# A narrow attention's stacks through DRAM: parts side by side, 12 reads of 4 KB rows and 6 writes a batch in place of 32 reads and one write

## The reference, cut to what matters

```python
def _L3_xattn_ref(query, key, value, Wq, bq, Wk, bk, Wv, bv, Wo, bo):
    EMBED_DIM, NUM_HEADS = 128, 16
    HEAD_DIM = EMBED_DIM // NUM_HEADS
    q = (query @ Wq.T + bq).reshape(b, tq, NUM_HEADS, HEAD_DIM).transpose(0, 2, 1, 3)
    k = (key @ Wk.T + bk).reshape(b, tk, NUM_HEADS, HEAD_DIM).transpose(0, 2, 1, 3)
    v = (value @ Wv.T + bv).reshape(b, tk, NUM_HEADS, HEAD_DIM).transpose(0, 2, 1, 3)
    scores = jnp.einsum('bhqd,bhkd->bhqk', q, k) / np.sqrt(HEAD_DIM)
    attn = jax.nn.softmax(scores, axis=-1)
    out = jnp.einsum('bhqk,bhkd->bhqd', attn, v)
    return out.transpose(0, 2, 1, 3).reshape(b, tq, EMBED_DIM) @ Wo.T + bo
```

## Time and profile before

| what | value |
|---|---|
| time, median of 3 runs | 2500.98 us (2495.63 to 2509.0) |
| the profiled execution | 2520.08 us, its span 2518.3 us, mean granted TensorE clock 0.896 |
| busy | TensorE 79% of the span, VectorE 61%, ScalarE 52%, GpSimd 20% |
| transfers scratch<-parts (L1408) | 768 of 32 KB |
| transfers parts<-scratch (L1398) | 24 of 384 KB, median 2.6 us from issue to landing |
| the three narrow attentions, first write issued at | 376.17, 1085.53 and 2177.64 us |

### The profile page before, as it was taken

One profiled execution on the slowest core, in us unless ns is written; L12 is line 12 of the kernel. 1 busy time (PEld: TensorE's weight loads), 2 busy tenths in 40 slices (PEclk: granted clock), 3 DMA queues, 4 the chain that ended last, 5 costly groups with the idle time before them and its releaser, 6 DMA issues.

```text
span 2518.3 us, 40083 instructions
## 1 busy us (share of the span) xinstructions
PE 1995.4 (79%) x14307; PEld 1343.5 (53%) x14307; DVE 1543.5 (61%) x3577; ACT 1305.5 (52%) x2677; POOL 491.1 (20%) x531
## 2 busy tenths in 40 slices
PE   6999766879999999848763288999999997488756
PEld 4666552447777777513351154566656676234435
DVE  6877675756666666357566825666665455578412
ACT  4666433657777777326653135666665212256412
POOL 2111012104232233142013431010000001211143
PEclk9999876989999999858986588999999898699878
DMA  4000003310000000023110000000000100332212
GB/s 175 1 1 2 1 5 94 79 43 1 1 1 1 1 1 1 1 76 80 31 69 1 0 9 1 1 1 1 1 1 1 51 1 1 120 85 60 64 40 70
DMA packets 83302, 73.90 MB, mean 29 GB/s; under 512 B 8633, under 2 KB 76361, under 8 KB 82081
## 3 DMA queue, kind: packets, MB, share of 16 engines
q1 hardware_dynamic: 81313, 68.95, 9.5%
q0 software_dynamic: 1792, 2.38, 0.3%
HBM read 54.73 MB, written 17.62 MB: 29 GB/s over the span
## 4 chain that ended last, share of the span: by engine, by line
PE 50%; DVE 22%; SPq 8%; issue 7%; ACT 7%; DMA 3%; another core or an unknown queue 1%; POOL 1%; DVEq 0%; ACTq 0%; POOLq 0%
PE bank L468 42%; SPq L1408 8%; DMA scratch<-parts 2%; DVE w_keep L1921 1%; PE bank L652 1%; PE bank L368 1%; PE bank L2868 1%; DVE stats L245 1%; ACT w_early L3109 1%; PE bank L692 1%; DVE w_early L2532 1%; DVE scratch L1225 1%; DVE scratch L3007 1%; DVE scratch L720 1%
## 5 line engine op out<-in xcount | busy, mean ns | idle before, releaser
L468 PE MATMUL bank<-scratch 64*128 64x256 bf16 (+5 forms) x3664 | 397.7, 323 | 122.1 <-DMA scratch<-parts 84.3
L468 PEld LDWEIGHTS bank<-scratch 64*128 64x128 bf16 (+3 forms) x3664 | 221.1, 123 | 268.8 <-issue 80.7
L1225 DVE TENSOR_REDUCE scratch<-bank 128x2 f32<-128x512 f32 x384 | 245.9, 686 | 128.9 <-PE bank L468 126.0
L468 PE MATMUL bank<-w_keep,scratch 128*128 128x128 f32 (+4 forms) x1760 | 246.4, 332 | 35.5 <-ACT scratch L805 20.8
L1311 ACT ACTIVATE w_keep<-bank 128x512 f32<-128x512 f32 x384 | 210.2, 596 | 98.3 <-PE bank L468 92.6
L468 PE MATMUL bank<-XNT,w_keep 128*128 128x256 f32 (+4 forms) x800 | 237.2, 435 | 7.2 <-POOL w_keep L2169 2.4
L468 PEld LDWEIGHTS bank<-w_keep,scratch 128*128 128x128 f32 (+3 forms) x1760 | 184.1, 185 | 97.3 <-issue 46.3
L468 PE MATMUL bank<-w_early,scratch 128*128 128x128 f32 (+4 forms) x1184 | 170.7, 350 | 34.2 <-DVE X L3388 19.2
L3109 ACT ACTIVATE w_early<-bank,scratch 128x256 f32<-128x256 f32 x256 | 123.7, 563 | 131.0 <-DVE scratch L3011 131.0
L468 PEld LDWEIGHTS bank<-XNT,w_keep 128*128 128x128 f32 x800 | 148.8, 196 | 60.7 <-issue 29.4
L468 PEld LDWEIGHTS bank<-w_early,scratch 128*128 128x128 f32 (+4 forms) x1184 | 127.6, 191 | 91.2 <-issue 63.3
(11 more groups left out here) (438 smaller groups left out, 3781.0 us busy)
## 6 DMA issues: line engine op xcount, KB each, us to landing
scratch<-parts SPq DMA_DIRECT2D x768, 32.0 KB
parts<-scratch SPq DMA_DIRECT2D x24, 384.0 KB, 2.6
w_early<-pack_l3f SPq DMA_DIRECT2D x1, 4758.0 KB, 14.9
w_keep<-pack_l2f SPq DMA_DIRECT2D x1, 2124.0 KB, 12.9
w_early<-pack_mamba SPq DMA_DIRECT2D x1, 2120.0 KB, 19.1
w_keep<-pack_l2x SPq DMA_DIRECT2D x1, 2049.0 KB, 8.2
w_keep<-taps SPq DMA_DIRECT2D x4, 512.0 KB, 5.2
w_early<-wave_kernels SPq DMA_DIRECT2D x1, 2048.0 KB
```

Of the source, the lines that this page charges most:

```text
L468: return pe.matmul(out, lhsT, rhs, start=start, stop=stop, skip_group_check=True)
L1225: dve.tensor_reduce(neg[:, :, h], self.k.bank[5 - g % 2][:, :].rearrange("p (t s) -> p t s", s=S), AXX, ALU.max, negate=True).then_inc(*s. ...
```

## The change

The DRAM buffer is laid out anew: for each part, for queries and for keys, a block of 16 rows (8 features of the even heads, 8 of the odd ones), a row holding the 8 heads of its kind side by side, 256 tokens each, 4 KB. Each block is written by a transfer of its own, 128 pieces of 512 B, six a batch; the two of a part are issued as soon as that part is cut. The eight pairs are the same, in another order: (0,0) (0,1) (0,2), (1,0) (1,1) (1,2), (2,0) (2,1). The tables now hold runs (first part, step, count), and one read fills the places of a run, 24 or 16 rows of 4 KB: three reads for each of queries and keys, even and odd heads, 12 a batch. The source of a read is count x 8 rows x 4 KB, with a step of 0 between the parts of a query's run.

```diff
-QUERY_PARTS = (0, 0, 1, 1, 0, 2, 1, 2)
-KEY_PARTS = (0, 1, 0, 1, 2, 0, 2, 1)
+QUERY_PARTS = ((0, 0, 3), (1, 0, 3), (2, 0, 2))
+KEY_PARTS = ((0, 1, 3), (0, 1, 3), (0, 1, 2))
...
         k, s = self.k, self.k.s
+        wide = H // 2
         for b in range(B):
             dram = k.parts_dram[b % 2]
-            sp.wait_ge(*s.pool.at("cut", b, 3))
             if b >= 2:
                 sp.wait_ge(*s.loaded_stack((b - 2) % 3).at(b - 2))
-            sp.dma_start(dram, self.pieces[b % 2]).then_inc(*s.parts_out.up(b))
+            for c, made in enumerate((0, 2, 3)):
+                sp.wait_ge(*s.pool.at("cut", b, made))
+                for n in range(2):
+                    place = bass.AP(dram.tensor, dram.offset + (c * 2 + n) * P * S, [[S, wide], [wide * S, 2 * HD], [1, S]])
+                    sp.dma_start(place, self.part(b, c)[:, n * S:(n + 1) * S]).then_inc(*s.parts_out.up(*((b,) if (c, n) == (2, 1) else (b, c, n))))
             if b >= 3:
                 sp.wait_ge(*s.scored.at("s", (b - 2) * H - 1))
             sp.wait_ge(*s.parts_out.at(b))
-            view = self.stacks[b % 3].rearrange("p (n w s) -> p n w s", n=2, s=S)
-            for n, parts in enumerate((QUERY_PARTS, KEY_PARTS)):
+            for n, groups in enumerate((QUERY_PARTS, KEY_PARTS)):
                 for o in range(2):
-                    for j, c in enumerate(parts):
-                        row, last = HW * o + HD * j, (n, o, j) == (1, 1, HD - 1)
-                        src = bass.AP(dram.tensor, dram.offset + HD * o * 6 * S + c * 2 * S + n * S, [[6 * S, HD], [2 * HD * 6 * S, H // 2], [1, S]])
-                        sp.dma_start(view[row:row + HD, n, :, :], src).then_inc(*s.loaded_stack(b % 3).up(*((b,) if last else (b, n, o, j))))
+                    row = HW * o
+                    for i, (first, step, count) in enumerate(groups):
+                        last = (n, o, i) == (1, 1, len(groups) - 1)
+                        src = bass.AP(dram.tensor, dram.offset + (first * 2 + n) * P * S + o * HD * wide * S,
+                                      [[step * 2 * P * S, count], [wide * S, HD], [1, wide * S]])
+                        there = self.stacks[b % 3][row:row + count * HD, n * wide * S:(n + 1) * wide * S]
+                        sp.dma_start(there, src).then_inc(*s.loaded_stack(b % 3).up(*((b,) if last else (b, n, o, i))))
+                        row += count * HD
```

## The result

The change makes the kernel slower: 2645.9 us against 2498.3, ratio 1.058, 95% interval 1.055 to 1.061. The forecast was 2596 in a range of 2530 to 2690, slower with 0.83. The sign and the mechanism came out as forecast. The amount did not: +95 us were forecast, on a median of 2501, and +147.6 measured, so the time lies 50 us above the forecast.

The account below looks back on a forecast made before the run. Three attentions were taken as bound by a loop of issue to usable stack plus TensorE's leg, not an engine. Their added +32.2, +31.4 and +31.4, together +95 us on the median of 2501, gave 2596 us, range 2530 to 2690.

Parts of the forecast that it names:

- the turn: Steady loop of a batch in the three attentions: issue to usable stack plus TensorE's leg, 17.1 + 4.6 = 21.7 us.
- TensorE's leg: TensorE's steps from usable stack until the next reads can be issued: 4.6 us at low clock (3.0 to 5.5).
- time from first issue to usable stack: From a batch's first read issue to its first matmul: 15.2 us of data plus 1.9 of latency, 17.1 us.
- Issue of the reads: SyncE issuing a batch's reads: 12 in place of 32, 4.2 us in place of 11.1, hidden under the data.
- the six writes: Writes of a batch's parts, queued behind reads: 2.3 us of data; their issue, 2.1 us, in SyncE's idle time.
- Engines of a read: DMA engines carrying a batch's reads: three for eight reads, two for four, always the same first ones.
- The reads' data: Transfer of a batch's stack: 96 rows of 4 KB on the first engine, 15.2 us (14.6 to 18.7).
- The second loop: Reads of a batch, next batch's writes behind them, then its reads: 19.4 us (18.8 to 24.9), setting batches 1 and 2.
- The sum: One attention from batch 0's first read to batch 7's usable stack: 164.4 us; together +95 us over three attentions.
- What follows batch 7: The rest of the kernel after an attention's last stack: stays as it is, no added time.
- split by the destination's rows: Rival: reads spread by the destination's 24 or 16 rows over 12 or 16 engines, -55 us, 2446 us; chance 0.13.
- No worse than now: Rival: three engines, but data in 12.1 us at 32 GB/s an engine, so no change, 2500 us; chance 0.04.

Follow-up runs that it names:

- e5: On top of e1, query parts written in copies and key parts interleaved, so ten of 12 reads have like shapes: 2476.1 us, ratio 0.983 to the kernel before.
- e1: The change with the source's two outer dimensions swapped, feature outside, giving eight engines a read: 2459.6 us, ratio 0.985 to the kernel before.
- e3: The change's layout, writes and product order, but each run read place by place in 32 reads of 8 rows: 2497.3 us, ratio 0.999 to the kernel before.
- e2: The change with other tables only, four runs of two parts, 16 reads on two engines: 2754.4 us, ratio 1.102 to the kernel before.
- e4: The change with 24 unused matmuls ahead of each wait for a stack from batch 1 on: 2624.7 us, ratio 1.051 to the kernel before.
- e6: The kernel before with only its write of a batch's parts split into six, first two issued early: 2525.1 against 2520.4 us, ratio 1.0024.

## Why the prediction was right, point by point

The path was right: reads on three and two engines, always the same first ones, bind the turn together with TensorE's leg at the low clock. What was mis-sized is the time from first issue to usable stack, 17.1 us where the steady turns have 18.9, and to a smaller part the leg.

- **Issue of the reads**: forecast 12 x 0.349 = 4.2 us, measured 8.5. The step that priced an issue by the earlier trace rows failed: all transfers there have like shapes, and the change's have not (0.70 against 0.36 in e5). It cost the change nothing, since the data takes longer. The same step failed for the six writes: forecast 2.1 us, measured 6.9 to 8.5 in the change, where one of the six stands over 2 us, and 3.7 in e1; in the change it ends before the reads have landed (397.20 against 399.78 in batch 0), in e3 it binds. In e1 the reads' issue is what makes the stack usable after 10.3 us.
- **Engines of a read**: three and two, confirmed by the share of 0.18, by the 32 small packets of a batch, by e2 (0.13) and by e1 (eight). The 77 GB/s that were to go with it were read as 68: eight reads on three and four on two are 2.67 engines in the mean, 69 GB/s at 25.9 each. The Trainium skill, page "DMA: Bandwidth & Descriptors", section "Why a DMA increments its semaphore by 16 and not by 1", gives the largest number up to 16 that divides the slowest dimension above 1 of both sides; the traces agree for 3 against 24, 2 against 16 and 8 against 24 and 16, which no row of before showed.
- **The reads' data**: forecast 15.2 us and 17.1 to the usable stack; measured 18.0 in the first batch, and 18.4 to 19.6 in the steady turns of all three attentions, 18.9 in the mean. Here the sum was too small. The latency around the data is not the cause: by the trace's packets the first row begins 1.55 us behind the first issue and the last one ends 0.5 ahead of the first matmul, 2.1 us for 1.9. The rate is right for most rows, 159 or 160 ns in the median, 25.8 GB/s. But of a batch's 256 rows some 13 took over 220 ns, up to 1.2 us, and nearly all of these lie in the first 9.8 us behind the first issue (296 of 307). So the mean row took 173 ns, 15 more than the forecast's, which over 96 rows is 1.4 us: the data took 15.9 us in the first batch, and 16.4 to 17.5 in the steady ones. The six writes, a near suspect since they run beside the second half of the reads, are not to blame: rows in that half took 163 ns in the mean, those ahead of it 183, and batch 7, which has no writes behind it, needs 18.7, 19.4 and 18.6 us like the batches before it. What makes the few rows slow stays open.
- **The second loop** (reads, writes behind them, reads): forecast 19.4, measured 20.1 (381.79 to 401.91) and 20.3. It sets batches 1 and 2, as forecast: the next reads are issued 2.1 us after the stack is usable (399.78 to 401.91), so the last write did land behind the reads. In e3 the same order of transfers binds, filled by SyncE's issue.
- **TensorE's leg**: forecast 4.6, measured 4.6 to 5.0 in the first two attentions and 5.4 to 5.5 in the third, at clock 0.50; only the first leg of each attention, behind batch 2's stack, was shorter, 3.9 to 4.3. e4 shows that it is the clock.
- **The sum**: a turn of 24.0 in place of 21.7, 1.9 of it in the time to the usable stack and 0.3 in the leg. Over the first attention 1.6 us too little in the first two turns, 1.4 at batch 2's stack, 9.1 in four steady turns, 1.6 at the last stack, and 0.7 too much in the first leg: 177.5 where 164.4 was forecast. That is 13.1 us, 39 in three such attentions; the three measured ones miss 43 of the 50 us. What follows batch 7, costed at nothing, has a leg at low clock as well, some 6 us over the three.
- **The rivals**: "split by the destination's rows" would have given 2446, and e1 shows that it was the right thing to fear for the other sign: with eight engines the same edit gives 2460. "No worse than now" needed 32 GB/s from an engine, and no row of before gave over 27.0; the change's own rows gave 25.8.

## What to carry to other kernels

Fewer and larger transfers are not faster by themselves: look at the slowest dimension of both sides, since the largest number up to 16 that divides both decided here how many DMA engines work, and put a dimension of 8 or 16 outermost even if it is not the largest stride. When a transfer's time is cut, look for the second loop through the same queue (here the next batch's writes behind the reads) before expecting the gain, and price its issue too. A wait that grows on TensorE's path costs again behind it, at the lower clock: here 1.6 to 2.5 us a turn, legs of 4.6 to 5.5 us in place of 3.0.

## What the runs showed that was not expected

SyncE took 0.58 to 0.70 us to issue a read whose two sides have different shapes (medians 0.67 in the change, 0.64 in e1, 0.58 in e2; 0.70 in e5), and 0.30 to 0.38 for one with like shapes (medians 0.31 before and 0.30 in e3, for reads of 32 KB; 0.34 to 0.38 in e5, for 64 and 96 KB); some 0.04 us of gap come to each. The writes differ less: 0.57 us with different shapes (e3), 0.43 with like ones (e6). Twelve such issues took 8.2 to 8.5 us, 32 of the other kind 10.8 to 11.1: cutting the number of transfers from 32 to 12 saved 2.6 us of issue, not 6.9.
